# An adaLN block on one core: x loaded row by row, the v projections one stage later, the adapter's factors split once

## The reference

```python
x = hidden                                        # 1 x 1024 x 512, float32
mod = silu(c) @ wmod                              # 512 -> 6 * 512: sa, ca, ga, sb, cb, gb
ga, gb = sign(ga) * max(|ga|, 0.25), the same for gb
h = layernorm(x) * (1 + ca) + sa
q, k, v = h @ wq.T + bq, h @ wk.T + bk, h @ wv.T + bv   # per token 32 heads of 16
probs = softmax(einsum("shd,std->sht", q, k) / 4)       # 32 x 32 per token: heads against heads
x = x + ga * einsum("sht,std->shd", probs, v)
h = layernorm(x) * (1 + cb) + sb
b = one of 8 blocks of 128 tokens
delta = h @ (A_eff[b].T B_eff[b].T + A_shared.T B_shared.T)  # A_eff, B_eff: sums of 16 adapters, by gate
x = x + gb * (h @ kernel + bias + delta)
```

## Time and profile before

| | |
|---|---|
| time, three runs | 259.19, 259.36 (median), 263.77 us |
| profiled execution | 258.68 us, its span 256.9 us |
| mean granted TensorE clock | 0.947 |
| busy in the span: PE, DVE, POOL, ACT | 195.3, 118.7, 104.6, 97.9 us |
| DMA | 27.9 MB, 109 GB/s over the span |

### The profile page before, as it was taken

One profiled execution on the slowest core, in us unless ns is written; L12 is line 12 of the kernel. 1 busy time (PEld: TensorE's weight loads), 2 busy tenths in 40 slices (PEclk: granted clock), 3 DMA queues, 4 the chain that ended last, 5 costly groups with the idle time before them and its releaser, 6 DMA issues.

```text
span 256.9 us, 3292 instructions
## 1 busy us (share of the span) xinstructions
PE 195.3 (76%) x1290; PEld 161.8 (63%) x1290; DVE 118.7 (46%) x180; ACT 97.9 (38%) x170; POOL 104.6 (41%) x71
## 2 busy tenths in 40 slices
PE   0000099999599995059999999926999979599995
PEld 0000099988388884056888879924898458377675
DVE  3111220282852001136678603877048978698431
ACT  4000020700943940300683545666355190546440
POOL 6000000295000893000089853897501848265640
PEclk9999999999799999657999999995799999999999
DMA  1129941116785109950299599985260022211212
GB/s 14 51 72 300 245 116 50 54 51 223 306 120 48 1 1 248 263 188 1 52 133 136 91 121 147 322 160 165 36 129 4 0 61 64 82 41 49 77 42 82
DMA packets 29152, 27.90 MB, mean 109 GB/s; under 512 B 16432, under 2 KB 20784, under 8 KB 28496
## 3 DMA queue, kind: packets, MB, share of 16 engines
q1 hardware_dynamic: 29136, 27.69, 47.6%
HBM read 17.20 MB, written 2.10 MB: 75 GB/s over the span
## 4 chain that ended last, share of the span: by engine, by line
PE 46%; SPq 18%; DVE 9%; POOL 9%; issue 6%; DMA 6%; ACT 3%; DVEq 0%
SPq L324 11%; PE ps L980 10%; PE ps L982 9%; PE ps L981 9%; DMA x<-_attn_hidden_states_dram 5%; PE ps L1065 4%; PE ps L972 3%; SPq L334 3%; PE ps L1101 3%; DVE xres L906 3%; POOL ctx_c L487 3%; SPq L329 2%; PE ps L1151 2%; POOL steps L473 2%; POOL steps L480 2%
## 5 line engine op out<-in xcount | busy, mean ns | idle before, releaser
L999 PE MATMUL ps<-silu,wm_attn 128*128 128x1 f32 x64 | 13.8, 352 | 31.9 <-DMA wm_attn<-in_L_wmod_dram 31.9
L446 POOL TENSOR_TENSOR hT_lo<-h_full,hT_hi 128x512 fp32r<-128x512 f32 x8 | 10.2, 1292 | 67.1 <-ACT hT_hi L570 67.0
L999 PEld LDWEIGHTS ps<-silu,wm_attn 128*128 128x128 f32 x64 | 13.7, 332 | 31.9 <-issue 31.9
L473 POOL TENSOR_TENSOR steps<-steps,rmax 128x1024 f32<-128x1024 f32 x8 | 15.3, 1928 | 35.8 <-DVE rmax L850 35.8
L558 ACT ACTIVATE std<-mv 128x2 f32<-128x2 f32 (+1 forms) x6 | 1.2, 202 | 54.4 <-DVE mv L759 54.4
L809 DVE SCALAR_TENSOR_TENSOR wm_sum<-wm_next,silu,wm_sum 128x2048 f32<-128x2048 f32 x3 | 7.1, 2352 | 29.6 <-DMA wm_next<-in_L_wmod_dram 29.6
L487 POOL TENSOR_TENSOR ctx_c<-ctx_c,ga_col 128x512 f32<-128x512 f32 x8 | 12.1, 1531 | 17.8 <-DVE ctx_c L874 17.8
L754 DVE BATCH_NORM_STATS2 stats<-x 128x6 f32<-128x512 f32 x8 | 5.4, 690 | 28.0 <-DMA x<-_attn_hidden_states_dram 28.0
L578 ACT ACTIVATE k<-ps,b_col 128x512 f32<-128x512 f32 x8 | 8.7, 1208 | 25.3 <-PE ps L982 14.0
L537 POOL TENSOR_TENSOR b_lo<-b_cat,b_hi 64x512 fp32r<-64x512 f32 x8 | 10.2, 1277 | 19.4 <-ACT b_hi L685 19.4
L480 POOL TENSOR_TENSOR steps<-steps,rinv 128x1024 f32<-128x1024 f32 x8 | 15.4, 1923 | 2.8 <-DVE rinv L860 2.8
(11 more groups left out here) (128 smaller groups left out, 502.8 us busy)
## 6 DMA issues: line engine op xcount, KB each, us to landing
wm_next<-in_L_wmod_dram SPq DMA_DIRECT2D x3, 1024.0 KB, 10.9
x<-_attn_hidden_states_dram SPq DMA_DIRECT2D x16, 128.0 KB
wm_attn<-in_L_wmod_dram SPq DMA_DIRECT2D x4, 512.0 KB, 17.5
diag<-k SPq DMA_DIRECT2D x16, 128.0 KB, 4.8
q<-q SPq DMA_DIRECT2D x16, 128.0 KB, 7.8
diag<-v SPq DMA_DIRECT2D x8, 256.0 KB, 9.0
xres<-_attn_hidden_states_dram SPq DMA_DIRECT2D x2, 1024.0 KB, 8.0
out_dram<-xres SPq DMA_DIRECT2D x7, 256.0 KB, 2.0
```

The source lines that it names most:

```text
L473: nc.gpsimd.tensor_tensor(rows, rows, rmax[:, c % 2 * RCH:(c % 2 + 1) * RCH].unsqueeze(2).to_broadcast([P, RCH, H]), ALU.subtract).then_in ...
L999: ins = nc.tensor.matmul(dst[:, n * IC + c:n * IC + c + 1], wm_attn[:, c, n * P:(n + 1) * P], silu[:, 2 * IC + c:2 * IC + c + 1], start=Tr ...
```

## The change

- x: one transfer per block of 128 tokens, a token per partition, in the order of memory. The rows of the diagonal tiles (`row`) and the quarters of v are renumbered to fit.
- v of half 0 is projected where v of half 1 was, between `scores(0)` and `scores(1)`; v of half 1 follows `scores(1)`, ahead of `context(0)`. The second half of h is transposed right after k of half 0.
- SP's order: `gate_col` ahead of the k copies; quarters 2 and 3 of the modulation ahead of the q copies of half 0; the FFN kernel behind the q copies of half 1; the second x and the adapter's factors behind the v copies of half 0.
- The FFN kernel is split behind softmax 1, ahead of the context's removal from PSUM; `b_eff` is done ahead of `context(1)`; the tail and `b_raw` are split once (two passes on ACT and two on POOL, and one each for the tail), and SP copies the finished high and low parts: 2 + 16 copies into `b_hi`, and behind the end of `context(1)` 1 + 8 into `b_lo`. VectorE no longer takes context tiles between the chunks of softmax 1; the first four normalisations for h2 come ahead of the second half's context.
- Tiles get other places in SBUF (left out below): among others `k0` and `k1` now share one, and so do `q0` and `v0`.

```diff
@@ bank_plan: the order in which PSUM banks are taken
+    uses += [("h_t", i, "a") for i in half(1, IC)]
     uses += [("q", i, "a") for i in range(2)]
     uses += [("wv_t", i, "v") for i in range(IC)]
     uses += [("q", i, "a") for i in range(2, IC)]
-    uses += [("h_t", i, "a") for i in half(1, IC)]
-    uses += [("v", i, "a") for i in half(0, IC)]
     uses += [("k", i, "a") for i in range(IC, IC + 2)]
...
     uses += [("q", i, "a") for i in half(1, IC)]
+    uses += [("v", i, "a") for i in half(0, IC)]
+    uses += [("scores", s, "a") for s in half(1, NSH)]
     uses += [("v", i, "a") for i in half(1, IC)]
-    uses += [("scores", s, "a") for s in half(1, NSH)]
     uses += [("ctx", s, "v") for s in half(0, NSH)]
...
     uses += [("ctx_t", i, "v") for i in half(0, NCT)]
+    uses += [("b_eff", 0, "a"), ("b_eff", 1, "a")]
     uses += [("ctx", s, "v") for s in half(1, NSH)]
-    uses += [("b_eff", 0, "a"), ("b_eff", 1, "a"), ("h2_t", 0, "a"), ("h2_t", 1, "a")]
+    uses += [("h2_t", 0, "a"), ("h2_t", 1, "a")]
...
@@ row numbers of the diagonal
         def row(s, a):
-            return (s * STACK + a) * D
+            return (s % 2 * SLOT + s // 2 * STACK + a) * D
...
@@ sync: x
-            x_abg = x[0].rearrange("(j b a g) n -> j a b g n", b=SIDE, a=STACK, g=NG2)
             def load_x(j):
-                for a in range(STACK):
-                    sp.dma_start(xn[j // NBH][GP * a:GP * (a + 1), j % NBH, :], x_abg[j, a]).then_inc(x_in[j], 16)
+                sp.dma_start(xn[j // NBH][:, j % NBH, :], x_rows[:, j, :]).then_inc(x_in[j], 16)
...
             sp.dma_start(bs_nat, lora_bs.rearrange("(c p) r -> p c r", p=P)).then_inc(lsh_in, 16)
+            for n in range(NG):
+                for c in range(IC):
+                    sp.dma_start(gate_col[rank * n:rank * (n + 1), c * NB:(c + 1) * NB],
+                                 gate[:, NG * c + n].partition_broadcast(rank),
+                                 allow_slow_non_contiguous=True).then_inc(gate_in, 16)
...
@@ sync: the order of the copies
             k_to_diagonal(0)
-            for n in range(NG):
-                for c in range(IC):
-                    sp.dma_start(gate_col[rank * n:rank * (n + 1), c * NB:(c + 1) * NB],
-                                 gate[:, NG * c + n].partition_broadcast(rank),
-                                 allow_slow_non_contiguous=True).then_inc(gate_in, 16)
             for c in (2, 3):
                 sp.wait_ge(wm_used, c - 1)
                 sp.dma_start(wm_next, wm[:, c, 2 * hid:6 * hid]).then_inc(wm_rest_in[c], 16)
-                if c == 2:
-                    q_to_diagonal(0)
+            q_to_diagonal(0)
             sp.dma_start(bias_bc[:], bias.partition_broadcast(P)).then_inc(bias_in, 16)
-
-            sp.wait_ge(psum_written, written("v", IC - 1))
-            sp.dma_start(chunked(kern_nat), kern.rearrange("(c p) n -> p c n", p=P)).then_inc(kern_in, 16)
+            k_to_diagonal(1)
             sp.wait_ge(ga_ready, 1)
             sp.dma_start(as_nat[0:rank, :], lora_as[:, :]).then_inc(lsh_in, 16)
-            k_to_diagonal(1)
+            sp.wait_ge(psum_written, written("scores", NSH - 1))
+            q_to_diagonal(1)
+            sp.wait_ge(k_diag_in[1], 16 * SLOT * STACK)
+            sp.dma_start(chunked(kern_nat), kern.rearrange("(c p) n -> p c n", p=P)).then_inc(kern_in, 16)
             v_to_diagonal(0)
-            q_to_diagonal(1)
+            sp.wait_ge(q_diag_in[1], 16 * SLOT * STACK)
+            sp.dma_start(xr[0], x_rows[:, 0:NBH, :]).then_inc(x_again[0], 16)
             sp.wait_ge(v_diag_in[0], 16 * QUAD)
             for c in range(IC):
                 sp.dma_start(lb_nat[:, c, :].rearrange("p (n r) -> p n r", r=rank),
                              lora_b[:, c * P:(c + 1) * P, :].rearrange("n p r -> p n r")).then_inc(lb_in, 16)
-            sp.wait_ge(k_diag_in[1], 16 * SLOT * STACK)
+            sp.wait_ge(psum_written, written("v", 2 * IC - 1))
             sp.dma_start(la_nat, lora_a.rearrange("(c n) r i -> (n r) c i", n=NG)).then_inc(la_in, 16)
-            sp.wait_ge(q_diag_in[1], 16 * SLOT * STACK)
-            sp.dma_start(xr[0], x_rows[:, 0:NBH, :]).then_inc(x_again[0], 16)
             v_to_diagonal(1)
...
             sp.wait_ge(psum_written, written("ctx", NSH - 1))
-            sp.wait_ge(tail_scaled, 1)
+            sp.wait_ge(tail_split, 1)
             shared = slice(rank, 2 * rank)
+            def tail_rows(src):
+                return src[shared, :].bitcast(F32).unsqueeze(1).to_broadcast([rank, NB, hid])
             for r0 in (rank, 3 * rank):
-                sp.dma_start(b_cat[r0:r0 + rank],
-                             b_tail[shared, :].unsqueeze(1).to_broadcast([rank, NB, hid])).then_inc(b_tail_in, 16)
+                sp.dma_start(b_hi[r0:r0 + rank].bitcast(F32), tail_rows(tail_hi)).then_inc(b_tail_in, 16)
...
             for b in range(NB):
-                q, r = b // NG, slice(rank * (b % NG), rank * (b % NG + 1))
+                r, q = own_rows(b)
                 if b % NG == 0:
-                    sp.wait_ge(b_scaled, q + 1)
+                    sp.wait_ge(b_split, q + 1)
                 for r0 in (0, 2 * rank):
-                    sp.dma_start(b_cat[r0:r0 + rank, b, :], b_raw[r, q, :]).then_inc(b_eff_in[b], 16)
+                    sp.dma_start(b_hi[r0:r0 + rank, b, :].bitcast(F32), b_raw_hi[r, q, :].bitcast(F32)).then_inc(b_eff_in[b], 16)
+            sp.wait_ge(psum_written, written("ctx", 2 * NSH - 1))
+            sp.dma_start(b_lo[shared].bitcast(F32), tail_rows(tail_lo)).then_inc(b_tail_in, 16)
+            for b in range(NB):
+                r, q = own_rows(b)
+                sp.dma_start(b_lo[0:rank, b, :].bitcast(F32), b_raw_lo[r, q, :].bitcast(F32)).then_inc(b_eff_in[b], 16)
...
@@ gpsimd
-            for j in range(NB):
-                if j == 1:
-                    scale_b(1)
-                pool.wait_ge(b_hi_made, j + 1)
-                nc.gpsimd.tensor_tensor(b_lo[0:2 * rank, j, :], b_cat[0:2 * rank, j, :],
-                                        b_hi[0:2 * rank, j, :].bitcast(F32), ALU.subtract).then_inc(b_split, 1)
...
+            pool.wait_ge(tail_hi_made, 1)
+            nc.gpsimd.tensor_tensor(tail_lo[r, :], b_tail[r, :], tail_hi[r, :].bitcast(F32),
+                                    ALU.subtract).then_inc(tail_split, 1)
...
+            for i in range(2):
+                pool.wait_ge(b_hi_made, i + 1)
+                nc.gpsimd.tensor_tensor(b_raw_lo[:, i, :], b_raw[:, i, :], b_raw_hi[:, i, :].bitcast(F32),
+                                        ALU.subtract).then_inc(b_split, 1)
+            for s in range(NSH, 2 * NSH, 2):
+                gate_ctx(s, 2)
...
@@ scalar
-            for i in range(IC):
-                project_v(i)
-            act.wait_ge(q_diag_in[0], 16 * SLOT * STACK)
             for i in range(IC, 2 * IC):
                 project("k", i, k_n, 0)
...
-            for i in range(IC, 2 * IC):
+            act.wait_ge(q_diag_in[0], 16 * SLOT * STACK)
+            for i in range(IC):
                 project_v(i)
...
-            ctx_low_part(0)
+            project_v(IC)
+            project_v(IC + 1)
             exp_chunk(2 * NCH - 1)
-            for s in range(1, NSH):
+            project_v(IC + 2)
+            project_v(IC + 3)
+            act.wait_ge(kern_scaled, 1)
+            nc.scalar.activation(kern_hi, kern_nat, ACT.Copy).then_inc(kern_hi_made, 1)
+            for s in range(NSH):
                 ctx_low_part(s)
...
-            act.wait_ge(kern_scaled, 1)
-            nc.scalar.activation(kern_hi, kern_nat, ACT.Copy).then_inc(kern_hi_made, 1)
+            act.wait_ge(psum_written, written("b_t", IC - 1))
+            act.wait_ge(tail_scaled, 1)
+            r = slice(rank, 2 * rank)
+            nc.scalar.activation(tail_hi[r, :], b_tail[r, :], ACT.Copy).then_inc(tail_hi_made, 1)
+            for i in range(2):
+                empty("b_eff", i, b_raw[:, i, :])
+            for i in range(2):
+                act.wait_ge(b_scaled, i + 1)
+                nc.scalar.activation(b_raw_hi[:, i, :], b_raw[:, i, :], ACT.Copy).then_inc(b_hi_made, 1)
             deviations(2, 0, 2)
+            deviations(3, 2, 4)
...
@@ vector
-                if c == 2 * NCH:
-                    ctx_high_part(0)
-                    ctx_high_part(1)
-                if c == 2 * NCH + 1:
-                    ctx_high_part(2)
-                    ctx_high_part(3)
                 if c > NCH + 1:
                     turn(c - 2)
-            for s in range(4, NSH):
+            dve.wait_ge(kern_hi_made, 1)
+            nc.vector.tensor_tensor(kern_lo, kern_nat, kern_hi.bitcast(F32), ALU.subtract).then_inc(kern_split, 1)
+            for s in range(NSH):
                 ctx_high_part(s)
...
@@ tensor
+            pe.wait_ge(xn_ready, XN_DVE)
+            h_t(1)
             pe.wait_ge(*emptied("wq_t", IC - 1))
...
-            pe.wait_ge(xn_ready, XN_DVE)
-            h_t(1)
```

(30 more changed lines are left out.)

110 lines of the change are left out of this document (45 added, 65 removed).

## The result

The changed kernel takes 228.94 us (median of four executions, 227.78 to 231.11), before 259.27: a ratio of 0.884 [0.875, 0.893]. The profiled execution took 227.78, its span is 226.0, 8.5 less than the 234.5 that the prediction had for it; of these, 2.3 lie ahead of the first scores, 1.9 between them and the adapter block, and 4.3 in that block. (Executions of one kernel lie up to 4% apart, with the mean granted clock of TensorE; the ratios here leave the slower group out, the medians do not.)

The account below looks back on a forecast made before the run. Late transfers were taken to bound much: slow x delaying TensorE's start, and gate_col holding SP's in-order queue ahead of wm_next. Front 87.7, rest 146.8 and 1.8 around the span sum to 236.3, say 236 us; range 222 to 247.

Parts of the forecast that it names:

- the loads: Front: x, modulation, wk, wq, wv and two wm quarters loaded by 36.1 us, bounds 33 and 41.
- E: Rival, x load: x stays slow because of what it reads and writes; S = 120.6, time 269; chance 0.05.
- S: Start of the first scores, end of the front: 87.7 us foretold, 124.4 before.
- L1041 to the scores: Front's last stretch (old line L1048), taken as 12.2 us as before.
- it isn't TensorE that decides there: At old L1048, TensorE ready by 69; the queue through gate_col, k copies and wm quarters decides, 75.4.
- B: Rival, front: gate_col doesn't hold the queue behind large loads; S = 79, time 228; chance 0.12.
- the 9.5 us lost here: Between S and h2: h2 begins at S + 90.2, before at 80.7; nearly as much as the v tiles take.
- the block: Adapter block, from its transposes at S + 60.5 to h2: 29.7 us, before 31.0 with 1.3 of waits.
- the 4.4 late shifts: Softmax 1: its shifts queue on GpSimd behind the FFN kernel's scaling, to S + 38.6, 4.4 us late.
- The wait for the b copies: Tail: first output product waits for b's copies until S + 101.7, 4.7 us late.
- C: Rival, after S: both new waits, FFN kernel and b copies, are hidden; 4.4 and 4.7 drop out, 227; chance 0.15.
- A: Main case, whole kernel: time as summed, 228 to 244 us; chance 0.55.

Follow-up runs that it names:

- experiment 1: Changed kernel with x loaded in its old reading order by 16 transfers: 265.69 us, 1.028; with x in new order as two 64-partition transfers per block: 233.28, 0.902.
- experiment 2: Changed kernel with gate_col filled from eight neighbouring elements per transfer: 229.46 us, 0.885; with each of gate_col's sixteen transfers issued twice: 245.99, 0.951.
- experiment 4: Changed kernel with the FFN kernel's load ahead of the second q copies: 224.87 us, 0.867; instead with second-half v ahead of the second scores: 238.42, 0.913.
- experiment 6: Changed kernel with 14 and 24 unread TensorE products in two front waits, for h of the second half and at L1041: 227.03 us, 0.866.
- experiment 5: Changed kernel with SP's b copies by halves, high parts, low tail and low parts of tiles 0 to 3 before those of 4 to 7: 229.56 us, 0.877.

## Why the prediction was right, and where it was off

**x, and TensorE's start.** Right in kind (experiment 1) and safe in size: x was priced at 263 GB/s and moved at 299 and more, so that the loads end at 32.5 and not 36.1, and the first weights are there at 9.4, not 11.5. E, the rival on the slower side, was the right thing to fear: with x slow the rest of the change costs 6.5 us (by E's mechanism S = 120.6 and 269 were foretold; with x put back S is 121.8 and the time 265.7).

**S.** 87.7 foretold, 85.4 measured, by the same links: loads -3.6, gate_col -0.7 (15.8), quarter 2's landing -0.9, quarter 3 +1.5 (7.3 instead of 5.85, for the q copies now go beside it), L1041 to the scores +1.4 (the clock). So terms of 5.2 less and 2.9 more cancel in part. The k copies took the 8.1 that they were priced at. The failed step is "it isn't TensorE that decides there", as far as it names gate_col alone: experiment 2 shows that k's emptying, which the prediction never put a time to, lets the copies go within 1 or 2 us of the same moment. With it the link would have read "the later of gate_col and k", and B, which the prediction gave 0.12 and 228, would have been seen to be worth next to nothing: without the cost of gate_col the scores start at 86.1, against 85.4 and 86.7 with it.

**The middle.** Scores 1, the kernel's load and scaling (done at S + 37.6, 38.6 foretold), the shifts held by it, context 0 and the last turn (S + 55.8, 56.9 foretold) came as summed; experiment 4 confirms that the kernel holds the shifts. One link is right, but not as it is worded: 8 and 4 us behind the end of the q copies' issue, 24.5, would be 36.5 and not 34. The q copies move from S + 20.7 on, soon after the first of them is issued, for 8 us, and the kernel lands at S + 32.9. And that the 9.5 us lost here are the price of the v tiles isn't borne out: with v of the second half ahead of the second scores the block comes 6.8 later still. What the 4.4 late shifts cost at the block is 2.8, since TensorE's own work ends only that much earlier. Mis-sized was kern_lo: 3.2 foretold from the earlier trace rows, 2.25 measured. In the trace of before (first line) it ran beside GpSimd's gating of the context, here (second line) GpSimd is idle, from 139.9 to 144.3:

```profile
200.13 5.79 POOL L487 TENSOR_TENSOR ctx_c<-ctx_c,ga_col 128x512 f32<-128x512 f32 x3 [1.60 <-DVE ctx_c L874]
```

```profile
141.13 2.25 DVE L897 TENSOR_TENSOR kern_lo<-kern_nat,kern_hi 128x2048 fp32r<-128x2048 f32 x1
```

**The block, 25.4 instead of 29.7.** This is the largest miss, half of the 8.5. The 29.7 was taken from a stretch of which 8 us ran at a clock of 0.50, that is 4 us of work at full clock: 29.7 - 4 = 25.7. The rows agree. The kernel before came to the transposes of the context here:

```profile
189.08 1.96 PE L972 MATMUL ps<-ident,ctx_c 128*128 128x128 f32 x16
```

That is 15.0 behind the block's first line, 13.3 without waits, where the changed kernel takes 9.5; from there to h2 either takes 16. The prediction saw the half clock and left it in, "which the block's 29.7 holds already", although the wait in front of it (5.2 before) was itself changed by the edit; it is 2.8 now and the clock stays at 1.00. The block of experiment 6, 1.7 longer behind a wait of 2.9 at a clock of 0.89, and that of experiment 4, 2.1 longer behind 10.7 idle us, show the term moving with the clock. In part this is chance: behind waits of 2.7 to 3.2 the block took 25.4 in three profiles and 27.0 in six (last section), so that 2.6 of the 4.3 are the change's and 1.7 hang on the execution.

**The tail.** The wait for the b copies (3.8, foretold 4.7), the first product 11.5 behind h2, the second tile at 22.0 (foretold 21.9) and the last 34.7 came out. The 10.5 from the first to the second tile's product are right by luck: before, they held a wait of 3.07 at a clock of 1.00, now one of 0.56 and a stretch at a low clock behind the 3.8 (0.71 from 181 to 191; the context's sixteen transposes take 3.68 there and took 2.08). And experiment 5 says that taking the 3.8 away needn't pay: C counted it as 4.7 won, and the times show 0 to 2.

The signs that were to show it all showed, with two other times: gate_col's stretch from 32.5, and TensorE from 9.4. Foretold was also that A would fall if the adapter block began before S + 56; it began at S + 58.6.

## What to carry to other kernels

A slow transfer that stands first in a queue is paid by everything behind it, and one edit that removes it can be worth more than the whole: undo edits one at a time before crediting any. Where one release seems to set a chain, put a time on the other things that the same instruction waits for; two that end within 2 us, as here, make either look free when it is taken away, and dear when it is doubled. A duration read from a stretch at half clock belongs to the idle time ahead of that stretch: when an edit changes the wait, take the duration at full clock and price the clock by itself, as a range: behind one and the same wait it may fall or not.
